# Projection weights in a contraction-first layout, and the values' products written out over rows in place

## The reference

```
B, S, HID = 64, 32, 512 ; D, HQ, HK = 128, 32, 8
q = einsum('bsd,ed->bse', x, Wq)        # Wq: (4096, 512)
k = einsum('bsd,ed->bse', x, Wk)        # Wk: (1024, 512)
v = einsum('bsd,ed->bse', x, Wv)        # Wv: (1024, 512)
q, k = rope(rmsnorm(q)), rope(rmsnorm(k))
o = softmax(q k_all^T * SCALE, masked) v_all     # 32 query heads, 8 key heads, 544 keys
out = x + einsum('bse,de->bsd', o, Wo)  # Wo: (512, 4096)
```

## Time and profile before

| | |
|---|---|
| median of 3 runs | 2462.31 us (2461.73 to 2463.17) |
| the profiled execution's own time | 2460.18 us |
| its span | 2458.0 us |
| busy: TensorE, VectorE, ScalarE, GpSimd | 96%, 72%, 55%, 47% |
| mean granted TensorE clock | 0.982 |

### The profile page before, as it was taken

The page is one execution under the profiler, slowest core; times in us unless marked ns, Lnnn a source line. Parts: engine busy times, 40 slices in busy tenths (PEclk is TensorE's granted clock), DMA queues, the critical chain, the costliest instruction groups (busy, mean ns, idle before and its releaser), DMA issues. The chain is left out here.

```text
span 2458.0 us, 51373 instructions
## 1 busy us (share of the span) xinstructions
PE 2359.9 (96%) x15297; PEld 1973.4 (80%) x15297; DVE 1774.6 (72%) x3412; ACT 1348.4 (55%) x2635; POOL 1152.9 (47%) x1362
## 2 busy tenths in 40 slices
PE   6988899999999499999999999999999997999999
PEld 5337777777777399999999999999999997888887
DVE  4656288988889588888888888888888886432221
ACT  6653387788777355555555555555555554321111
POOL 0322134443444277767777777777776774000000
PEclk9999999999999699999999999999999999999999
DMA  9335323333232588888888888888888885743442
GB/s 315 98 102 180 90 80 93 108 108 103 90 107 86 171 274 297 293 292 276 295 288 296 279 287 297 292 289 278 292 295 297 272 293 183 211 126 99 133 137 60
DMA packets 470906, 501.43 MB, mean 204 GB/s; under 512 B 102069, under 2 KB 396981, under 8 KB 466742
## 3 DMA queue, kind: packets, MB, share of 16 engines
q1 hardware_dynamic: 433974, 366.37, 47.2%
q0 software_dynamic: 36864, 134.23, 15.6%
HBM read 404.02 MB, written 96.47 MB: 204 GB/s over the span
## 5 line engine op out<-in xcount | busy, mean ns | idle before, releaser
L1134 POOL TENSOR_TENSOR att_probs<-att_probs,att_inverse 128x512 f32<-128x512 f32 x512 | 536.0, 1047 | 288.6 <-DVE att_inverse L1330 284.0
L1238 ACT ACTIVATE att_probs<-att_probs,att_low 128x544 f32<-128x544 f32 x512 | 383.7, 750 | 515.3 <-DVE att_low L1317 452.0
L1195 PE MATMUL att_o<-att_probs_t,att_values 128*128 128x128 f32 x4096 | 540.9, 275 | 0.0
L1317 DVE CUSTOM_DVE_ANT_0 att_probs<-att_score,att_mask,att_batch_cols 128x544 f32<-128x544 f32 x512 | 400.0, 781 | 138.6 <-PE att_score L1160 99.9
L1195 PEld LDWEIGHTS att_o<-att_probs_t,att_values 128*128 128x128 f32 x4096 | 497.6, 192 | 0.0
L1326 DVE COPY att_probs_t<-att_turn 128x512 f32<-128x512 f32 x512 | 350.7, 685 | 1.2 <-PE att_turn L1175 1.2
L1120 POOL DMA_INDIRECT att_values<-L_cond_v_cache,att_v_rows_of x256 | 282.1, 1102 | 83.1 <-POOL att_v_rows_of L1116 48.8
L1160 PE MATMUL att_score<-att_keys_raw,att_queries_raw 128*128 128x288 f32 (+1 forms) x1024 | 290.7, 407 | 29.5 <-DMA att_queries_raw<-q_t 27.3
L1175 PE MATMUL att_turn<-ident,att_probs 128*128 128x128 f32 x2048 | 311.0, 274 | 1.2 <-POOL att_probs L1134 0.8
L1293 DVE TENSOR_TENSOR att_keys_lo<-att_keys_raw,att_keys_hi 128x384 fp32r<-128x384 f32 (+1 forms) x320 | 259.3, 811 | 17.6 <-ACT att_keys_hi L1231 17.6
L1175 PEld LDWEIGHTS att_turn<-ident,att_probs 128*128 128x128 f32 x2048 | 244.1, 141 | 33.3 <-POOL att_probs L1134 1.4
(11 more groups left out here) (140 smaller groups left out, 4103.1 us busy)
## 6 DMA issues: line engine op xcount, KB each, us to landing
att_keys_raw<-L_cond_k_cache SPq DMA_DIRECT2D x1024, 128.0 KB
q_t<-proj_q_out SPq DMA_DIRECT2D x32, 1024.0 KB, 3.9
att_queries_raw<-q_t SPq DMA_DIRECT2D x64, 512.0 KB
o_t<-att_heads_out SPq DMA_DIRECT2D x64, 512.0 KB, 6.6
out_o_raw<-o_t SPq DMA_DIRECT2D x32, 1024.0 KB, 5.7
prep_natural<-L_cond_weight SPq DMA_DIRECT2D x16, 1024.0 KB, 8.0
w_nat<-L_cond_Wq SPq DMA_DIRECT2D x8, 1024.0 KB, 5.8
v_new<-values_v_out SPq DMA_DIRECT2D x64, 128.0 KB, 2.1
```

Source lines behind the costliest of these rows:

```text
L1134: nc.gpsimd.tensor_tensor(probs[:, k, 0:L], probs[:, k, 0:L], inverse[:, k:k + 1].to_broadcast([P, L]), ALU.mult).then_inc(probs_ready, 1)
L1195: last = nc.tensor.matmul(o, values[j][:, t, h * D:(h + 1) * D], probs_t[m % 2][:, t * P:(t + 1) * P], start=(t == 0), stop=False, skip_gr ...
L1238: nc.scalar.activation(probs[:, k, :], probs[:, k, :], ACT.Exp, bias=low[k][:, 0:1], scale=-1.0, accum_out=total[k][:, 0:1]).then_inc(exp_ ...
L1317: nc.vector.tensor_tensor_reduce(out=probs[:, k, :], in0=score_ps[:, LEFT:LEFT + KEYS], in1=mask[j][:], scale=batch_cols[j][:, h:h + 1], s ...
```

## The change

The host hands over Wv, Wk, Wq and Wo with the contraction dimension first, in the tiles the kernel uses. All transposes of weights by TensorE, their PSUM banks and the semaphores that told of them go. ScalarE and VectorE split the weights straight from the loaded SBUF tiles. Loads that waited for a tile to be turned wait for it to be split. The loads of Wq and Wo have rows of 8 KB per partition, those of Wv 10 and 6 KB. In the values' stage the 16 groups are written out, TensorE reads its rows in `x3t_hi` and `x3t_lo` in place, and the slots and GpSimd's copies go. In the projection the product ring has five PSUM banks in place of four.

```
 stage_values
-            def chunk(rc, first):                       # GpSimd
-                pool.wait_ge(x3t_lo_ready, rc + 1)
...
-                        nc.gpsimd.tensor_copy(part[u][:], f32(x[:, :, bass.ds((rc * GC + gg) * P, P)])).then_inc(slot_ready[u], 1)
...
-                for c in range(IC):                     # TensorE
-                    last = nc.tensor.transpose(w_ps[h % BANKS][:, c * P:(c + 1) * P], rows[:, c * P:(c + 1) * P], ident[:])
-                last.then_inc(w_turned, 1)
             pe.wait_ge(w_ready, HK)
...
+            for g in range(G):
+                u, before = g % U, g // U
+                if g % GC == 0:
+                    pe.wait_ge(x3t_lo_ready, g // GC + 1)
+                if g >= U:
+                    pe.wait_ge(v_ready[u], before * 2)
+                rows = slice(g * P, (g + 1) * P)
+                for n in range(2):
+                    for c in range(IC):
+                        for k, (x, w) in enumerate(((x3t_hi, wvt_hi), (x3t_hi, wvt_lo), (x3t_lo, wvt_hi))):
+                            last = nc.tensor.matmul(v_ps[2 * u + n][:], x[:, c, rows], w[:, c, n * 512:(n + 1) * 512],
+                                                    start=(c == 0 and k == 0), stop=(c == IC - 1 and k == 2))
+                last.then_inc(v_done[u], 1)
...
             def split_weights(h):                       # ScalarE; VectorE likewise
-                act.wait_ge(w_turned, h + 1)
-                nc.scalar.activation(wvt_hi[:, :, h * D:(h + 1) * D], w_ps[h % BANKS].rearrange("p (c e) -> p c e", c=IC),
+                if h == WV_EARLY:
+                    act.wait_ge(wv_loaded, 16)
+                nc.scalar.activation(wvt_hi[:, :, h * D:(h + 1) * D], wv_rows(h).rearrange("p (c e) -> p c e", c=IC),
 load_head_weights
-    sp.dma_start(w_nat[:, 0, :], wk[bass.ds(h * D, D)]).then_inc(loaded, 16)
-    sp.dma_start(w_nat[:, 1:, :], wq[bass.ds(h * (REP * D), REP * D)].rearrange("(m p) i -> p m i", p=P)).then_inc(loaded, 16)
+    sp.dma_start(w_nat[:, 0, :], wk[bass.ds(h, 1)].rearrange("h p c e -> p (h c e)")).then_inc(loaded, 16)
+    sp.dma_start(w_nat[:, 1:, :], wq[bass.ds(h, 1)].rearrange("h p m c e -> p (h m) (c e)")).then_inc(loaded, 16)
 stage_projection
-        RING = 4
+        RING = 5
...
-                    sp.wait_ge(w_turned, M)
-                    sp.wait_ge(w_turned, h * M + M)
+                    sp.wait_ge(w_ready, M)
+                    sp.wait_ge(w_ready, h * M + M)
...
-                    if rc == 1 and not last_head:
-                        turn_weights(h + 1, 1 - u, m)
-
-            for m in range(M):
-                turn_weights(0, 0, m, True)
...
-                act.wait_ge(w_turned, h * M + (m + 1))
-                nc.scalar.activation(w_hi[u][:, m].rearrange("p c e -> p (c e)"), w_ps[(u * M + m) % 2][:],
+                if m == 0 and not first:
+                    act.wait_ge(w_loaded, h * 32)
+                nc.scalar.activation(w_hi[u][:, m].rearrange("p c e -> p (c e)"), w_nat[:, m, :],
...
-                nc.vector.tensor_tensor(w_lo[u][:, m].rearrange("p c e -> p (c e)"), w_ps[(u * M + m) % 2][:],
+                nc.vector.tensor_tensor(w_lo[u][:, m].rearrange("p c e -> p (c e)"), w_nat[:, m, :],
 stage_output
-                sp.dma_start(wo_nat[v][:], wo.rearrange("(c p) e -> p c e", p=P)[:, :, h * (REP * D):(h + 1) * (REP * D)]
+                sp.dma_start(wo_raw[v][:], wo[bass.ds(h, 1)].rearrange("h p r o -> p (h r) o")).then_inc(wo_loaded[v], 16)
...
-                sp.wait_ge(turned, (h - 1) * REP)
+                sp.wait_ge(w_ready, (h - 1) * REP)
...
-            turn_weights(0)
             for h in range(HK):
-                if h < HK - 1:
-                    turn_weights(h + 1)
                 pe.wait_ge(w_ready, (h + 1) * REP)
...
+                act.wait_ge(wo_loaded[h % 2], 16 * (h // 2) + 16)
                 for r in range(REP):
-                    act.wait_ge(turned, h * REP + (r + 1))
-                    nc.scalar.activation(wot_hi[:, h * REP + r, :], w_ps[r][:], ACT.Copy).then_inc(w_hi_ready, 1)
+                    nc.scalar.activation(wot_hi[:, h * REP + r, :], wo_raw[h % 2][:, r, :], ACT.Copy).then_inc(w_hi_ready, 1)
 host
+LAYOUTS = {
+    "L3_cond_k_cache": lambda a: a.transpose(0, 3, 2, 1),
+    "L3_cond_Wv": lambda a: a.reshape(HK, D, IC, P).transpose(3, 0, 2, 1),
+    "L3_cond_Wk": lambda a: a.reshape(HK, D, IC, P).transpose(0, 3, 2, 1),
+    "L3_cond_Wq": lambda a: a.reshape(HK, REP, D, IC, P).transpose(0, 4, 1, 3, 2),
+    "L3_cond_Wo": lambda a: a.reshape(HID, HK, REP, D).transpose(1, 3, 2, 0),
+}
```

More of the change, by code:

```diff
@@ L469, in stage_values @@
     GC = G // RC
-    BANKS = 4
     with ExitStack() as ctx:
@@ L512, in stage_values, with wv_rows @@
         block = ctx.enter_context(nc.Block())
+        def wv_rows(h):
+            return w_nat[:, h] if h < WV_EARLY else wv_nat[:, h - WV_EARLY]
         def split_all(split_weights, split_rows):
@@ L559, in _ @@
             pool.wait_ge(iotas, 1 + PPT)
-            def chunk(rc, first):
-                pool.wait_ge(x3t_lo_ready, rc + 1)
-                for gg in range(GC):
-                    u = gg % U
-                    if gg >= U or not first:
-                        pool.wait_ge(v_done[u], rc * (GC // U) + gg // U)
-                    for part, x in ((slot_hi, x3t_hi), (slot_lo, x3t_lo)):
-                        nc.gpsimd.tensor_copy(part[u][:], f32(x[:, :, bass.ds((rc * GC + gg) * P, P)])).then_inc(slot_ready[u], 1)
@@ L570, in _ @@
-            chunk(0, True)
-            with pool.Fori(1, RC) as rc:
-                chunk(rc, False)
         @block.tensor
         def _(pe):
-            for h in range(HK):
-                if h == WV_EARLY:
-                    pe.wait_ge(wv_loaded, 16)
-                rows = w_nat[:, h] if h < WV_EARLY else wv_nat[:, h - WV_EARLY]
-                if h >= BANKS:
-                    pe.wait_ge(w_ready, h - BANKS + 1)
-                for c in range(IC):
-                    last = nc.tensor.transpose(w_ps[h % BANKS][:, c * P:(c + 1) * P], rows[:, c * P:(c + 1) * P], ident[:])
-                last.then_inc(w_turned, 1)
@@ L585, in _ @@
-            pe.wait_ge(w_ready, HK)
-            def chunk(rc, first):
-                for gg in range(GC):
-                    u, before = gg % U, rc * (GC // U) + gg // U
-                    pe.wait_ge(slot_ready[u], before * 2 + 2)
-                    if gg >= U or not first:
-                        pe.wait_ge(v_ready[u], before * 2)
-                    for n in range(2):
-                        for c in range(IC):
-                            for k, (x, w) in enumerate(((slot_hi, wvt_hi), (slot_hi, wvt_lo), (slot_lo, wvt_hi))):
-                                last = nc.tensor.matmul(v_ps[2 * u + n][:], x[u][:, c, :], w[:, c, n * 512:(n + 1) * 512],
-                                                        start=(c == 0 and k == 0), stop=(c == IC - 1 and k == 2))
-                    last.then_inc(v_done[u], 1)
@@ L787, in _ @@
         def _(pe):
-            def turn_weights(h, u, m, first=False):
-                if m == 0 and not first:
-                    pe.wait_ge(w_loaded, h * 32)
-                n = (u * M + m) % 2
-                if m >= 2 or not first:
-                    pe.wait_ge(w_ready, h * M + (m - 1))
-                for c in range(IC):
-                    last = nc.tensor.transpose(w_ps[n][:, c * P:(c + 1) * P], w_nat[:, m, c * P:(c + 1) * P], ident[:])
-                last.then_inc(w_turned, 1)
             def sum_k(h, rc):
@@ L1462, in _ @@
         def _(pe):
-            def turn_weights(h):
-                pe.wait_ge(wo_loaded[h % 2], 16 * (h // 2) + 16)
-                for r in range(REP):
-                    if h:
-                        pe.wait_ge(w_ready, (h - 1) * REP + (r + 1))
-                    for c in range(IC):
-                        last = nc.tensor.transpose(w_ps[r][:, c * P:(c + 1) * P], wo_nat[h % 2][:, c, r * D:(r + 1) * D], ident[:])
-                    last.then_inc(turned, 1)
             def products(rc, h, first):
```

31 lines of the change are left out of this document (9 added, 22 removed).

## The result

| | before | after |
|---|---|---|
| median on the same chip | 2462.74 us (4 runs, 2461.73 to 2464.03) | 2430.85 us (4 runs, 2430.70 to 2431.79) |
| profiled execution's own time, its span | 2460.18, 2458.0 us | 2430.95, 2429.2 us |
| mean granted TensorE clock | 0.982 | 0.981 |

The ratio after to before is 0.9871 (95% interval 0.9854 to 0.9888): 31.9 us or 1.3% faster. The forecast was 2431.7 us.

What follows compares the result with a forecast made beforehand. TensorE, busy 96% of the span, was taken as the bound, so removed transposes count one for one: 0 + 3.8 + 16.0 + 10.5 + 0.3 = 30.6 us off 2462.31 gives 2431.7 us; range 2426 to 2439.

Steps and rivals of the forecast that it cites:

- The steady part: Projection after its start: five turned tiles cost 2.29 us a head, seven heads, 16.0 us gained; lower bound 12.3.
- The output stage: Output products: six blocks of 16 transposes, 1.75 us each, lie between the first chunk's products; 10.5 us gained.
- The start of the projection: First projection product 4.4 us sooner, less 0.6 for the slow clock: net 3.8 us gained, 2.2 if the clock rises late.
- The values' stage: First value product again at 196.15, since VectorE's split of head 7 sets it: 0 us; clock bound 1.7 us.
- slots and loop: Values' stage: GpSimd's copies wait for TensorE and the loop shows no gap, so removing both is worth 0.
- The output's start: Attention output rounded 1.0 us sooner, ahead of the first output product; 0.7 lost to the cold clock, net 0.3 us.
- The step that failed: Projection: VectorE, 1.4 us late in chunk 1, catches up in the other three chunks; the longer ring adds 3.15 us room.
- nothing reaches TensorE: Projection: with L889's split delayed by the median, VectorE's lateness does not hold up TensorE's products.
- VectorE late: Rival, projection: splits collide with GpSimd's additions and lateness reaches TensorE; 2437.3 us, or 2447.7 at worst; chance 0.10.
- Rows of 8 KB: Rival, weights' loads: such rows served by fewer engines, weights late; 2480.7 us at 22 us a load; chance 0.03.
- The further gain at the starts: Rival, values and output starts: faster 8 KB-row loads save 2 us each, cold starts stay short; 2426.4 us; chance 0.06.
- Doesn't do what it says: Rival, whole kernel: the transposes were hidden, so the time stays at 2462 us; chance 0.03.

Runs made afterwards that it cites:

- two more differences: Kernel after the change, with VectorE taking each weight tile's difference twice more in chunk 1 of every head, into a spare tile: 2490.40 us; with four product banks 2489.37 us.

## Why the prediction was right, and where its reasons were not

**The steady part** was given 16.0 us from the marks of the earlier trace rows and measured 16.05. The choice between the marks' 2.29 us a head and the 1.75 of the tiles' own delay was decided rightly by the neighbouring chunks. **The output stage** was given 10.5 less 0.7 for the clock, 9.8 us, and its products are 10.0 shorter. **The start of the projection** was given 4.4 and measured 4.3; the clock's part was put at 0.6 and measured 0.5. The timeline of that start, beside the earlier trace rows:

```profile
293.61 2.71 ACT L804 ACTIVATE proj_w_hi<-w_nat 128x512 fp32r<-128x512 f32 x5 [4.25 <-PEq L470]
294.27 3.10 DVE L847 TENSOR_TENSOR proj_w_lo<-w_nat,proj_w_hi 128x512 fp32r<-128x512 f32 x5 [38.04 <-ACT proj_w_hi L804]
295.11 0.77 PE L787 MATMUL proj_proj<-x3t_hi,proj_w_hi 128*128 128x512 f32 x1 [6.88 <-DVE proj_w_lo L847]
```

ScalarE splits the first tile at once, and the first product starts 1.50 us behind it; the sum of the earlier trace rows in the prediction had 1.4.

**The values' stage** was given 0. In this pair of profiles it cost 0.5: the first product starts 0.4 us later behind the maps, the products take 0.1 longer. But the two lengths together are 106.0 us in the kernel before and 106.1 and 106.8 in the two others that have its values' code, against 106.5 after, so 0.5 can't be told from 0. The chain is as described, the rows' rounding and then the lo parts of heads 5 to 7, which now stand behind the rows' lo part in one group:

```profile
193.04 1.91 ACT L588 ACTIVATE x3t_hi<-x3t_lo 128x2048 fp32r<-128x2048 f32 x1 [4.95 <-DMA x3t_lo<-x_cols]
...
194.98 2.29 DVE L622 TENSOR_TENSOR x3t_lo<-x3t_lo,x3t_hi 128x2048 fp32r<-128x2048 f32 x1 [5.84 <-ACT x3t_hi L588]
197.19 1.89 DVE L616 TENSOR_TENSOR values_wvt_lo<-values_wv_nat,values_wvt_hi 128x512 fp32r<-128x512 f32 x3
```

That slots and loop are worth 0 was right within a microsecond; 0.8 of the microsecond is the three splits from SBUF, which take 2.71 us beside the slot copies and 1.89 without them.

**The output's start** was the term furthest off in proportion: 1.0 us was given, 1.7 measured. The two other kernels with the old output code have 18.24 and 19.16 us there in place of 18.71, so the gain lies between 1.2 and 2.1. The loads of the attention output landed at 2068.9, 8.1 us after issue, and they alone end the wait; the weights were ready.

**Not foreseen**: 2.6 us lost ahead of the values' stage, in a profile where the clock rose later in the maps (full from 69.8 us in place of 66.5). The predicted terms come to 31.1 us (16.05 + 10.0 + 4.3 - 0.5 + 1.7 - 0.5) against 30.6, and the 28.8 between the spans is that less these 2.6, with some 0.3 gained around the attention stage and at the end. The runs' medians differ by 31.9. The profiled execution of the kernel before, 2460.18 us, was 2.6 under its own median, that of the kernel after only 0.1 off it; so these 2.6 are no loss in the medians. The moments that the prediction named moved with them: 196, 292 and 2071 us were named for the first products of the values, the projection and the output, and 199.1, 295.1 and 2073.3 came. Errors of opposite sign, the 0.5 and the 0.7 us at two starts, cancel in the sum, and the closeness of 2430.85 to 2431.7 owes that much to chance.

**The step that failed** is one that came to 0 in the sum: that VectorE, 1.4 us late in chunk 1, works it off where "it has 2.0 us each", and that the ring gives TensorE room. The windows of four chunks after show how little there is (the fourth figure group is VectorE's busy time):

```profile
383.62:399.35 15.73, 15.73 (x71) 11.71 (x70) 15.66 (x19) 13.66 (x24) 7.90 (x5) 1.00 0.19 62
399.35:415.08 15.73, 15.73 (x71) 11.72 (x70) 15.48 (x18) 12.00 (x21) 7.21 (x5) 1.00 0.30 97
415.08:430.83 15.75, 15.75 (x72) 11.73 (x71) 15.52 (x17) 12.21 (x21) 7.45 (x6) 1.00 0.32 92
430.83:446.56 15.73, 15.73 (x72) 11.72 (x71) 15.28 (x17) 13.25 (x23) 7.42 (x6) 1.00 0.54 173
```

VectorE's room is 0.07 to 0.45 us in a chunk and 1.2 in a head, not 4.6. Its busy time is not a fixed amount of work: the same 66 instructions took 3.4 us more, and the rows show where: the two rotation lines take 10.5 to 10.7 us a head over their 0.68 each where it was 6.9 to 7.1, and the additions beside the splits last 1.65 to 1.69 us where it was 1.28 to 1.31. The prediction put 58.30 us for VectorE's head, with 63.7 as its bound; it priced GpSimd's addition only on the instruction that was edited (L889), which stayed at 680 ns, and not on its neighbours (1.77 us where it was 1.41). That "nothing reaches TensorE" was right, but not by the ring: TensorE waits at the sums of squares when ScalarE is late, and there was just enough time before these. The fifth bank has no part in it (four give the same time; the loss at two more differences is the same with four). "VectorE late" did not happen but was near: five more instructions of 0.68 us in a head bring it about and turn the gain into a loss.

**The other rivals.** Rows of 8 KB did not make the projection's loads slow: the DMA issues give 5.4 us from issue to landing in place of the 5.8 in the earlier trace rows. The loads of Wo, also in rows of 8 KB now, took 7.1 us, where before the median was 5.7; they ended no wait of TensorE, and whether the rows or the shorter steps between the loads made them longer was not tested:

```profile
w_nat<-L_cond_Wq SPq DMA_DIRECT2D x8, 1024.0 KB, 5.4
...
out_wo_raw<-L_cond_Wo SPq DMA_DIRECT2D x8, 1024.0 KB, 7.1
```

The further gain at the starts did not come from these loads either. It is there to be had, though, and larger than that rival put it, by waiting for less (10.6 us) and keeping the clock up (4.9 us). "Doesn't do what it says" was excluded by the marks.

## What to carry to other kernels

When work is taken off the bounding engine, read the next engine's busy time again after the edit, chunk by chunk. Here the same 66 instructions went from 58.30 to 61.71 us: instructions beside GpSimd's additions take up to 1.79 us in place of 0.68, and what the two rotation lines take over their 0.68 went from some 7 us a head to 10.6 when an operand moved from PSUM to SBUF and the moments at which the instructions meet moved with it. After an edit that only swaps an operand's place, look at the durations of the instructions beside and behind it on both engines, not at its own. And at the start of each stage ask what the first product really needs; here that was worth a third of what removing all the transposes gave.

## What the runs showed of the hardware

- An addition of GpSimd that starts 0.15 us into a VectorE instruction with two SBUF inputs takes 1.66 us in place of 1.29 (with one input in PSUM it stayed at 1.30), and that instruction keeps its 0.68; the next one of VectorE with two SBUF inputs ends 0.55 us after the addition and takes up to 1.79 us in place of 0.68. One more instruction ahead of the split moved the price onto it (median 680 to 1776 ns).
- At three stage starts the granted clock was 0.50 over the first 3 us, and products of 512 columns started 0.43 us apart in place of 0.23. With transposes without use in the waits it was 1.00, and the kernel was 4.9 us faster. Where these transposes ran until just before the first product, the gap ahead of it was 1.8 us longer (16.56 against 14.79).
- In a stage whose code is unchanged the clock was full from 69.8 us in place of 66.5, and the stage ended 2.6 us later; over fourteen profiles its length was 124.8 to 127.2 us. A difference of that size between two profiles is no evidence about an edit elsewhere.
